# Self-attention scores and outputs issued for sixteen heads at a time, over the row and column strips of TensorE

## What is computed

```python
x = x + tanh(g_xattn) * cross_attention(layernorm(x), ctx)      # 16 heads of 128
h0 = layernorm(x)
# the gated block: all in fp32
h = rms(h0, w_ln1)
q, k, v = h @ wq + bq, h @ wk + bk, h @ wv + bv                   # 16 heads of 32, S = 100
q, k = rope(q, k)
scores = einsum('bqhd,bkhd->bhqk', q, k) * 32 ** -0.5
attn = softmax(where(causal, scores, min))
ctx = einsum('bhqk,bkhd->bqhd', attn, v)
x1 = h0 + ctx @ wo
h = rms(x1, w_ln2)
routed = top2_of_8_experts(h)                                     # inner size 352
shared = (silu(h @ w_sh_gate) * (h @ w_sh_up)) @ w_sh_down * sigmoid(h @ w_sh_eg)
return x + tanh(g_ffn) * (x1 + routed + shared)
```

## Time and profile before

| | us |
|---|---|
| three executions, median (lowest to highest) | 1025.49 (1020.36 to 1029.56) |
| the profiled execution's own time | 1027.2 |
| its span in the profile | 1025.4 |
| first scores of the self-attention to its last outputs | 522.9 to 665.8 |

### The profile page before, as it was taken

The page is one execution under the profiler, slowest core; times in us unless marked ns, Lnnn a source line. Parts: engine busy times, 40 slices in busy tenths (PEclk is TensorE's granted clock), DMA queues, the critical chain, the costliest instruction groups (busy, mean ns, idle before and its releaser), DMA issues.

```text
span 1025.4 us, 16190 instructions
## 1 busy us (share of the span) xinstructions
PE 938.4 (92%) x5713; PEld 860.4 (84%) x5713; DVE 661.9 (65%) x1484; ACT 573.1 (56%) x1441; POOL 427.8 (42%) x408
## 2 busy tenths in 40 slices
PE   4899999999999999989799999999888989989974
PEld 4889999999989999979678777798888988878863
DVE  3557776734657777602979747376746788888813
ACT  3656666645556666633455556444335777777711
POOL 3432222246522222466665442255372555554510
PEclk9999999999999999989989999699899999999996
DMA  4762000045500000053321110033578899999953
GB/s 132 209 232 79 1 1 1 1 135 148 158 29 16 1 1 2 8 140 96 89 77 42 43 42 21 12 93 95 177 217 227 266 272 309 285 275 297 276 101 104
DMA packets 125824, 120.76 MB, mean 118 GB/s; under 512 B 12380, under 2 KB 96292, under 8 KB 125144
## 3 DMA queue, kind: packets, MB, share of 16 engines
q1 hardware_dynamic: 107350, 97.73, 31.2%
q10 hardware_dynamic: 13978, 13.41, 4.8%
q0 software_dynamic: 4416, 8.58, 4.4%
HBM read 102.16 MB, written 17.53 MB: 117 GB/s over the span
## 4 chain that ended last, share of the span: by engine, by line
PE 59%; DMA 14%; DVE 14%; ACT 5%; issue 4%; POOL 2%; SPq 1%; ACTq 0%; POOLq 0%; DVEq 0%
PE bank L1978 52%; DMA eraw<-in_L_ffn_w_down_e_dram 5%; PE bank L2105 3%; DVE we L1304 3%; DMA s_sum<-yo,target 2%; ACT we L867 2%; DMA raw<-in_L_xattn_Wq_dram 1%; PE bank L2252 1%; DMA s_rows<-HR,idx 1%; DMA raw<-in_L_ffn_w_sh_down_dram 1%; DVE wf L1304 1%; DVE PQ L1483 1%; DMA raw<-in_L_ffn_wq_dram 1%; POOL wx L1831 1%; DVE PQ L1481 1%
## 5 line engine op out<-in xcount | busy, mean ns | idle before, releaser
L1860 POOL TENSOR_SCALAR SC<-SC,mx,anyv 100x361 f32<-100x361 f32 x128 | 81.4, 646 | 215.4 <-DVE mx L1417 204.3
L867 ACT ACTIVATE we<-eraw 128x704 fp32r<-128x704 f32 (+2 forms) x140 | 97.3, 719 | 34.6 <-DMA eraw<-in_L_ffn_w_down_e_dram 16.9
L1843 POOL TENSOR_TENSOR we<-eraw,we 128x704 fp32r<-128x704 f32 x40 | 71.1, 1779 | 104.2 <-ACT we L867 104.1
L1831 POOL TENSOR_TENSOR wx<-raw,wx 128x512 fp32r<-128x512 f32 x64 | 82.7, 1300 | 74.4 <-ACT wx L853 74.1
L1304 DVE TENSOR_TENSOR we<-eraw,we 128x704 fp32r<-128x704 f32 (+2 forms) x100 | 92.9, 946 | 24.4 <-ACT we L867 24.2
L1978 PE MATMUL bank<-H2h,wf 128*128 128x400 f32 x352 | 100.7, 353 | 0.0
L1831 POOL TENSOR_TENSOR wf<-raw,wf 128x512 fp32r<-128x512 f32 x54 | 73.6, 1371 | 57.5 <-ACT wf L853 57.5
L982 ACT ACTIVATE SC<-SC,mx 100x361 f32<-100x361 f32 x128 | 75.4, 593 | 27.2 <-DVE mx L1413 26.7
L853 ACT ACTIVATE wf<-raw 128x512 fp32r<-128x512 f32 x100 | 61.4, 626 | 48.7 <-DMA raw<-in_L_ffn_w_sh_down_dram 31.0
L1978 PE MATMUL bank<-XTh,wx 128*128 128x400 f32 x256 | 72.3, 356 | 4.3 <-POOL wx L1831 3.0
L1304 DVE TENSOR_TENSOR Kl<-bank,Kh 128x362 fp32r<-128x362 f32 x64 | 34.2, 535 | 60.2 <-ACT Kh L940 60.2
(11 more groups left out here) (265 smaller groups left out, 2899.6 us busy)
## 6 DMA issues: line engine op xcount, KB each, us to landing
eraw<-in_L_ffn_w_gate_e_dram SPq DMA_DIRECT2D x40, 352.0 KB, 3.9
eraw<-in_L_ffn_w_up_e_dram SPq DMA_DIRECT2D x40, 352.0 KB, 5.6
eraw<-in_L_ffn_w_down_e_dram SPq DMA_DIRECT2D x40, 256.0 KB, 6.3
raw<-in_L_xattn_Wq_dram SPq DMA_DIRECT2D x32, 256.0 KB, 3.3
raw<-in_L_xattn_Wo_dram SPq DMA_DIRECT2D x32, 256.0 KB, 2.9
raw<-in_L_ffn_w_sh_gate_dram SPq DMA_DIRECT2D x22, 256.0 KB, 3.2
raw<-in_L_ffn_w_sh_up_dram SPq DMA_DIRECT2D x22, 256.0 KB, 3.1
s_rows<-Z SPq DMA_DIRECT2D x6, 800.0 KB
```

Of the source, the lines that this page charges most:

```text
L867: eng.activation(weights("e", u)[0:rows, 0, 0:n], eraw[u % 6][0:rows, 0:n], ACT.Copy).then_inc(sem("act_e"), 1)
L1831: eng.tensor_tensor(w[:, 1, :, :], raw[plan.raw[stream, u] % 4][:, :, :], f32(w[:, 0, :, :]), ALU.subtract).then_inc(sem("pool_w"), 1)
L1843: eng.tensor_tensor(w[0:rows, 1, 0:n], eraw[u % 6][0:rows, 0:n], f32(w[0:rows, 0, 0:n]), ALU.subtract).then_inc(sem("pool_e"), 1)
L1860: eng.tensor_scalar(sc, sc, m[:, 3, h:h + 1], anyv[:, b:b + 1], ALU.mult, ALU.mult).then_inc(sem("pool_p"), 1)
```

## The change

`f_scores` is now called once for four units, a quarter `q` of the 32 units (0 to 7: one batch, sixteen heads). It writes the mask into four banks (0, 1, 2 and 5: `score_bank`), and then sixteen score matmuls in the order c = 0 to 3 outside and i = 0 to 3 inside, so that neighbours lie in different row strips and different banks. It is called at the end of the steps n = 0, 4, 8, ... 28, and waits for `act_fe` of 4q, which is the last exponential of the quarter before. `f_out` is called once for four units, in the steps 7, 11, ... 35, with its sixteen matmuls in the same order over the four column strips of bank 4; `pe_fo` now counts quarters. DVE's `f_max` of unit n moves to the start of step n (from unit n+1 at its end). `PTf` has six buffers in place of three. Bank 5 leaves the ring of the other work, which has the banks 6 and 7 until `moe1`. The first scores now wait for all eight `dve_ht` (the evacuation of the last `turn`, which uses bank 5) and for four `dve_v`. The arithmetic is unchanged.

```diff
-        turned = [("dve_ht", 8), ("dve_x1", 7), ("dve_x1", 8)]
-        empty = {5 + i: turned[i] for i in range(3)}
+        empty = {6: ("dve_x1", 7), 7: ("dve_x1", 8)}
...
-        count, n, ring = {}, 0, [5, 6, 7]
+        count, n, ring = {}, 0, [6, 7]
...
-    PTf = E_.ring("PTf", 3, [T, 4, T])
+    PTf = E_.ring("PTf", 6, [T, 4, T])
...
+    score_bank = [banks[0], banks[1], banks[2], banks[5]]
...
             if u >= 0 and u % 4 == 3:
                 h, b = divmod(u // 4, HB)
-                act.wait_ge(sem("pe_fo"), u + 1)
+                act.wait_ge(sem("pe_fo"), u // 4 + 1)
...
         def self_attention(n):
-            if n == 0:
-                f_max(0)
+            if n < 32:
+                f_max(n)
             u = n - 3
             if 0 <= u < 32 and u % 2:
                 dve.wait_ge(sem("pe_ft"), u + 1)
-                if u >= 3:
-                    dve.wait_ge(sem("pe_fo"), u - 2)
-                eng.tensor_copy(flat(PTf[u % 3][:, :, :]), banks[3][0:T, 0:4 * T]).then_inc(sem("dve_ft"), 1)
+                if u >= 6:
+                    dve.wait_ge(sem("pe_fo"), (u - 6) // 4 + 1)
+                eng.tensor_copy(flat(PTf[u % 6][:, :, :]), banks[3][0:T, 0:4 * T]).then_inc(sem("dve_ft"), 1)
...
-            if n + 1 < 32:
-                f_max(n + 1)
...
-        def f_scores(u):
...
+        def f_scores(q):
+
+            h, b = divmod(q, HB)
+            bs = slice(b * T, (b + 1) * T)
             pe.wait_ge(sem("dve_rope"), 8 * (h + 1))
             pe.wait_ge(sem("pool_const"), CONST["causal"])
-            if u >= 3:
-                pe.wait_ge(sem("act_fe"), u - 2)
+            if q:
+                pe.wait_ge(sem("act_fe"), 4 * q)
             else:
-                pe.wait_ge(sem("dve_v"), u + 1)
-            mm(by_batch(bank[0:T, 0:4 * T]), identb[:, :], causb[:, :, :].broadcast_to([T, 4, T]), True, False)
+                pe.wait_ge(sem("dve_v"), HB)
+                pe.wait_ge(sem("dve_ht"), B)
+            for bank in score_bank:
+                mm(by_batch(bank[0:T, 0:4 * T]), identb[:, :], causb[:, :, :].broadcast_to([T, 4, T]), True, False)
             for c in range(4):
-                e = mm(bank[0:T, c * T:(c + 1) * T], QT[h][ps, c, bs], KT[h][ps, c, bs], False, c == 3)
-            e.then_inc(sem("pe_fs"), 1)
+                for i in range(4):
+                    ps = slice(32 * i, 32 * i + 32)
+                    e = mm(score_bank[i][0:T, c * T:(c + 1) * T], QT[h][ps, c, bs], KT[h][ps, c, bs], False, c == 3)
+                    if c == 3:
+                        e.then_inc(sem("pe_fs"), 1)
+
+        def f_out(q):
+
+            h, b = divmod(q, HB)
+            pe.wait_ge(sem("act_ft"), 2 * q + 2)
+            pe.wait_ge(sem("dve_ft"), 2 * q + 2)
...
+            for c in range(4):
+                for i in range(4):
+                    at = (4 * c + i) * FD
+                    e = mm(banks[4][32 * i:32 * i + 32, c * T:(c + 1) * T], V[h][:, b, at:at + FD],
+                           PTf[(4 * q + i) % 6][:, c, :], True, True)
+            e.then_inc(sem("pe_fo"), 1)
 
         def self_attention(n):
-            if n == 0:
-                f_scores(0)
-            if n + 1 < 32:
-                f_scores(n + 1)
...
+            if u >= 0 and u % 4 == 3:
+                f_out(u // 4)
+            if n % 4 == 0 and n < 32:
+                f_scores(n // 4)
```

More of the change, by code:

```diff
@@ L453, in banks @@
             elif s[0] == "moe1":
[L454 removed]
+                empty |= {0: ("act_fe", 32), 1: ("act_fe", 32), 2: ("act_fe", 32), 5: ("act_fe", 32), 3: ("dve_ft", 16), 4: ("dve_cx", 8)}
                 n, ring = 0, list(range(8))
@@ L1062, in self_attention @@
                 act.wait_ge(sem("pe_ft"), u + 1)
-                if u >= 3:
-                    act.wait_ge(sem("pe_fo"), u - 2)
-                eng.activation(flat(PTf[u % 3][:, :, :]), banks[3][0:T, 0:4 * T], ACT.Copy).then_inc(sem("act_ft"), 1)
+                if u >= 6:
+                    act.wait_ge(sem("pe_fo"), (u - 6) // 4 + 1)
+                eng.activation(flat(PTf[u % 6][:, :, :]), banks[3][0:T, 0:4 * T], ACT.Copy).then_inc(sem("act_ft"), 1)
             u = n - 4
@@ L1076, in self_attention @@
                     act.wait_ge(sem("pe_ft"), u - 3)
-                p, m, bank = PF[u % 4], sm[u % 4], banks[u % 3]
+                p, m, bank = PF[u % 4], sm[u % 4], score_bank[u % 4]
                 for c in range(4):
@@ L1500, in f_max @@
         def f_max(u):
-            m, bank = sm[u % 4], banks[u % 3]
+            m, bank = sm[u % 4], score_bank[u % 4]
             dve.wait_ge(sem("pe_fs"), u + 1)
@@ L2254, in self_attention @@
             u = n - 4
-            if u >= 0:
-                h, b, i = u // 16, u // 4 % HB, u % 4
-                if u % 2:
-                    pe.wait_ge(sem("dve_ft"), u // 2 + 1)
-                else:
-                    pe.wait_ge(sem("act_ft"), u // 2 + 1)
-                pe.wait_ge(sem("dve_v"), HB * (h + 1))
-                if u >= 4:
-                    pe.wait_ge(sem("dve_cx"), u // 4)
-                else:
-                    pe.wait_ge(sem("dve_ht"), B - 1)
-                for c in range(4):
-                    at = (4 * c + i) * FD
-                    e = mm(banks[4][32 * i:32 * i + 32, c * T:(c + 1) * T], V[h][:, b, at:at + FD], PTf[u % 3][:, c, :], True, True)
-                e.then_inc(sem("pe_fo"), 1)
+            if u >= 0 and u % 4 == 3:
+                f_out(u // 4)
+            if n % 4 == 0 and n < 32:
+                f_scores(n // 4)
         def po(h, m):
```

11 lines of the change are left out of this document (6 added, 5 removed).

## The result

The changed kernel takes 1018.21 us (median of 20 executions, 1014.17 to 1025.35), the kernel before beside it 1026.59 us (20 executions, 1020.36 to 1033.94). The ratio is 0.9908, with a 95% interval of 0.9887 to 0.9928. The change gains 0.9%, about 9 us. That is inside 1%, but clear of nothing, and nearer to the full-overlap rival (1013) than to the forecast of 1027.

The account below looks back on a forecast made before the run. The prediction took TensorE to bound the kernel (92% busy). Strips and handing round gave -10.2 us, low clock +9.8, together -0.4: 1027.2 to 1026.8, say 1027 us; range 1011 to 1046.

Parts of the forecast that it names:

- full-overlap rival: Scores and outputs: strips overlap wholly, 0.022 to 0.03 us per record, about 1013 us; chance 0.25, shared with a held clock.
- The pace: Score and output records over four strips: about 0.057 us each, so 32 records take 1.8 us.
- what the strips save on the path: Sum over the self-attention's quarters of steps, with other work in the gaps: -10.2 us with the clock of before.
- The bound below: Score and output records if all four strips overlap: a quarter of 0.0885 us, 0.022 per record.
- 12 to 15: Steps 12 to 15, with three value batches: 16.4 us in place of 18.3, -1.9.
- The list of the quarter: One quarter without other work, handed between TensorE, DVE, ACT and POOL: 11.1 us against 9.84.
- two rotations on DVE: Steps 8 to 11: two three-instruction rotations, each instruction about 0.57 us, stand in DVE's chain; 14.0 us in place of 14.3.
- The first wait: TensorE idle by 1 to 1.3 us behind each set of scores, released by the copy of DVE.
- The clock: Low-clock cost: three stretches in steps 4 to 23 (+5), steps 24 to 27 (+3.3), 28 to router (+1.5); sum +9.8.
- if the time changes outside of it: Sign that the prediction is wrong: time changes outside the stage from first scores to last outputs.
- the 10 that the prediction allowed itself: Sign that the prediction is wrong: the stage from first scores to last outputs not within 10 us of its 143.
- the rivals: Whole kernel: full overlap 1013 or held clock 1017 (0.25 together), no overlap 1044 (0.22), clock stays low about 1047 (0.10).

Follow-up runs that it names:

- Kernel 1: The changed kernel with the score loops exchanged, strip outside and column block inside, so four neighbours share a strip: 1027.75 us, 0.9982 to the kernel before.
- kernel 2: The changed kernel with the loops of the sixteen output matmuls exchanged, strip outside: 1022.46 us, 0.9924 to the kernel before.
- 4: The changed kernel with ACT making the exponentials of unit 4q+3 before it evacuates bank 4 (CXh): 0.9907 to the kernel before.
- Kernel 5: The changed kernel with DVE's copy and reciprocal first in steps 4q, then all four maxima of the quarter there: 1013.08 us, 0.983 to the kernel before.
- 14: The changed kernel run again unaltered, on the chip of the later runs: 0.9896 to the kernel before.
- Kernel 8: The changed kernel with scores issued for two units, two banks in reserve, and the maximum back at its old place: 1018.48 us, 0.9893 to the kernel before.
- 12: Scores issued for two units on the changed kernel, two banks in reserve, with the maximum of unit n at the front of step n: 0.9906 to the kernel before.
- 16: Scores issued for two units on the changed kernel, maximum of unit n+1 ahead of the reciprocal in step n: 1009.97 us, 0.9822 to the kernel before.
- kernel 9: The kernel before with DVE's maximum moved ahead of the reciprocal in each step, its unit unchanged: 1.0014 to the kernel before.
- 11: The kernel before with only the outputs issued for four units, and the maximum moved ahead of the reciprocal: 1017.18 us, 0.985 to the kernel before.
- kernel 3: The changed kernel with DVE's copy and reciprocal ahead of the maximum in the steps 4q: 1022.15 us, 0.9894 to the kernel before.
- kernel 7: The changed kernel with earlier maxima, last exponentials ahead of CXh and three masks issued early, plus nine redundant masks in each step 4q: 0.9885 to the kernel before.

## Why the prediction was wrong, and what in it was right

- **The pace is the step that failed.** The term of the sum that was mis-sized is what the strips save on the path (-10.2 us with the clock of before). The prediction chose 0.057 us per record because two records of one fp32 matmul lie in one strip and would serialise. Measured are 0.0229 and 0.021. In the starts of single records the next four follow 88 ns later, so within a strip records do queue, but the three other strips fill that time. The bound below, a quarter of the pace in the earlier trace rows, was the answer, and it alone takes 1.0 to 1.1 us off each set of 32 (1.8 us predicted from first to last start, 0.73 and 0.66 by the measured pace): 12 to 15 came out 2.5 us shorter than predicted, 20 to 23 also 2.5, 24 to 27 even 4.7 (that one in part since its low clock began late, at 621.5). The steps 16 to 19 came out 1.0 longer, with a low stretch of 6.8 us from 594.2 in them and a wait of 2.37 us, ended at 596.42, for weights that POOL prepares. Kernel 1 confirms it for the scores: 7.6 us go when only the order of the strips is undone. For the outputs no run shows it: kernel 2 loses 1.6 us, within the intervals. With the bound put in, the prediction would have come to its first rival's 1013, 5 us below the measured time.
- **Why 1013 wasn't reached.** The list of the quarter ended with outputs, `CXh`, exponentials. Where rotations stand between the steps, the path is ACT, POOL, the rotation and the maximum on DVE, then the exponentials: 8 to 11 took 1.1 us more than predicted and 4 to 7 2.0 more, of which 1.4 is the low clock in the masks and scores (3.21 us against 1.81). The prediction had priced "two rotations on DVE" by their own length, and not by what they wait for. Kernels 2 and 4 found no time in the outputs or in `CXh`. Kernel 5 found it in the maximum's place: another 0.8%, with an interval that ends below the changed kernel's in the result and overlaps that of its second run (14) at the edge. The gain showed in other quarters than I had expected.
- **The maximum's place** was treated as a pure move. It has two effects: it loses a step of lead, and its scaling no longer waits for POOL. Kernel 8 has the lead without the short scaling (0.9893), 12 the short scaling without the lead (0.9906), 16 both (0.9822). The short scaling alone is worth 0 on the kernel before (9) and 0.7 to 1.1% on top of a batch (11, 16). How much of the change's own 0.9% hangs on it was not measured by itself.
- **The first wait** behind the scores (1.1 to 1.3 us, by DVE's copy; 1.42 at 559.88) was right in place, and in the steps 4q without effect on the sum (kernel 3). So was DVE's wait for the scores ahead of its maximum: 2.3 to 3.0 us in four of the first five steps 4q, where the prediction had some 2.5. The list for the steps 12 to 15 adds up to 16.3, not 16.4.
- **The clock** was right in sign and about in size. Low time rose by 23 us; at 0.37 us for each that is 8.6 us, where the prediction had 9.8. At full cost it would be half, 11.5. In the two profiles the low time of the stage rose from 30.7 to 47.8 us. Behind the stage it rose from 27.4 to 42.0 and the length by 3.8, which looks like the sign "if the time changes outside of it". But kernel 9 has the scores and outputs of the kernel before, and its profile has 48.3 us of low time and 362.8 us of length behind the stage (its windows are shown at 9). So single profiles do not show a change there. The 0.37 is an association in the scatter, since no kernel here changed the clock alone (kernel 7 came closest).
- **The whole.** The stage is 13.6 us shorter, outside of the 10 that the prediction allowed itself. The time lies in the range, since that reached into the rivals. As an estimate, the median is 8.4 us lower and the clock took about 8.6, so the path gave about 17 where the prediction had 10.2. This 17 is a difference and was not measured by itself.

## What to carry to other kernels

Small matmuls that use a strip of the array each should be issued with neighbours in different strips. Here the pace rose by the whole factor in both directions and in fp32, but the time only by what stood on the path: 0.7% hung on the order of the scores and nothing measurable on that of the outputs. So look next for the order on the other engines, as that is what binds then. When the bound engine is relieved, go once through what each in-order queue now puts ahead of the critical piece (here a maximum behind a rotation that waits for GpSimd), and re-time moves that were worth nothing before. An engine that works less may also get a lower clock (23 us more at 1.2 GHz here, worth about 8.6); count that against the gain before it is promised. Where single executions scatter, plot their time against their clock first.

## What the runs showed of the hardware that I had not expected

- Strips overlap across a boundary even in the poor order: in kernel 1 three records of a strip start 4 to 6 ns from those of the next (576.456 and .462, 576.628 and .632, 576.717 and .721), and 32 records take 2.26 us. With the outputs' order undone it is 1.99 us.
- An operation on 100x4 elements (0.17 us) can take 2.68 us, to the end of three GpSimd operations in a row, of which two began after it.
- TensorE's clock fell to 1.2 GHz in the changed kernel at 539.6, 566.9, 594.2 and 621.5 us (the last for 23.9 us). Three of the falls lie inside a wait (2.67, 2.37 and 3.25 us long, ended at 540.18, 596.42 and 622.25), the one at 566.9 comes 1.8 us behind a wait of 2.15. The waits of 1.42 us that ended at 559.88 and 575.01 had no fall behind them. That the waits cause the falls is likely, but no run changed them alone. In kernel 2, with longer outputs, the clock stayed at 2.4 GHz in a place where the changed kernel lost it; that is one profile of each, but the mean low time points the same way (99.5 us against 106).
- A good half of the scatter between executions of one kernel goes with the clock: 0.37 us of time for each us at 1.2 GHz, correlation 0.78 over 218 executions.
